# Clearing the slot rows only behind each expert's last token, and sending the last pairs' rows in one go

## What is computed

```
x = x + tanh(g0) * layernorm(attention(layernorm(x), ctx, mask))
y = layernorm(x)
logits = y @ w_router                    # 1792 tokens x 8 experts
top_vals, top_idx = top_k(logits, 2)
probs = softmax(top_vals)
h = square(relu(y @ w_fc[e]));  out_e = h @ w_proj[e]
x = x + tanh(g1) * sum over the two experts of probs * out_e
```

## Time and profile before

| | us |
|---|---|
| median of 3 runs | 1195.04 (1194.09 to 1195.85) |
| the profiled execution | 1202.38 |
| its span, first to last instruction | 1200.3 |
| PE busy | 1130.6 (94%) |
| DVE busy | 862.1 (72%) |
| ACT busy | 664.2 (55%) |
| POOL busy | 156.8 (13%) |
| mean DMA rate | 82 GB/s |

### The profile page before, as it was taken

How to read it: one execution, slowest core, us unless ns; L and a number is a source line. 1 busy time by engine, 2 the same in 40 slices (tenths; PEclk the granted TensorE clock), 3 DMA queues, 4 the chain that set the end, 5 groups by cost and what they waited for, 6 DMA issues and landing times.

```text
span 1200.3 us, 56000 instructions
## 1 busy us (share of the span) xinstructions
PE 1130.6 (94%) x24824; PEld 1082.1 (90%) x24824; DVE 862.1 (72%) x2003; ACT 664.2 (55%) x846; POOL 156.8 (13%) x186
## 2 busy tenths in 40 slices
PE   4799999999999999999999999999999999969884
PEld 4799999999999999999999999999999999968874
DVE  4467776777777776777777777777777777757677
ACT  1466565655556565656565556656565656534432
POOL 0000100010010101010111101010101101023431
PEclk9799999999999999999999999999999999989998
DMA  4223132222323233323222232323321222124306
GB/s 153 74 74 91 57 93 79 85 76 77 91 88 91 67 87 93 80 63 94 83 86 68 89 91 88 87 71 87 93 78 50 79 61 71 30 54 120 90 25 169
DMA packets 59487, 98.57 MB, mean 82 GB/s; under 512 B 14514, under 2 KB 42034, under 8 KB 59250
## 3 DMA queue, kind: packets, MB, share of 16 engines
q1 hardware_dynamic: 49538, 79.55, 23.9%
q10 hardware_dynamic: 6832, 8.92, 2.1%
q0 software_dynamic: 2880, 6.53, 1.5%
HBM read 70.32 MB, written 24.71 MB: 79 GB/s over the span
## 4 chain that ended last, share of the span: by engine, by line
PE 86%; issue 5%; DVE 5%; DMA 2%; POOL 1%; ACT 1%; SPq 0%; DVEq 0%; POOLq 0%; ACTq 0%
PE v_ps L601 22%; PE k_ps L604 21%; PE sc_ps L627 20%; PE o_ps L642 13%; PE k_ps L659 1%; PE sc_ps L544 1%; PE sc_ps L545 1%; PE k_ps L666 1%; PE sc_ps L546 1%; PE v_ps L692 1%; DVE acc L1509 1%; DVE h_sq L1438 1%; DVE acc L1452 1%; POOL rstd L460 0%; PE k_ps L805 0%
## 5 line engine op out<-in xcount | busy, mean ns | idle before, releaser
L897 ACT ACTIVATE prob<-sc_ps,m_bias 125x896 f32<-125x896 f32 x384 | 377.9, 1009 | 329.7 <-PE sc_ps L627 329.3
L601 PE MATMUL v_ps<-wv_hi,c_hi 64*125 64x256 f32 x1520 | 312.0, 285 | 2.7 <-DVE c_lo L1066 2.6
L604 PE MATMUL k_ps<-c_hi,wk_hi 64*128 64x500 f32 x760 | 306.8, 404 | 0.0
L601 PE MATMUL v_ps<-wv_lo,c_hi 64*125 64x256 f32 x1520 | 302.1, 279 | 0.0
L601 PE MATMUL v_ps<-wv_hi,c_lo 64*125 64x256 f32 x1520 | 301.9, 278 | 0.0
L604 PE MATMUL k_ps<-c_lo,wk_hi 64*128 64x500 f32 x760 | 294.0, 387 | 0.0
L604 PE MATMUL k_ps<-c_hi,wk_lo 64*128 64x500 f32 x760 | 293.2, 386 | 0.0
L1075 DVE TENSOR_TENSOR vst<-v_ps,rowv 125x512 f32<-125x512 f32 x191 | 131.3, 687 | 184.9 <-PE v_ps L601 184.9
L1277 DVE TENSOR_SCALAR prob<-prob 125x896 f32<-125x896 f32 x384 | 235.5, 626 | 21.3 <-ACT prob L897 21.1
L601 PEld LDWEIGHTS v_ps<-wv_hi,c_hi 64*125 64x125 f32 x1520 | 227.0, 185 | 16.6 <-issue 5.7
L627 PE MATMUL sc_ps<-q_hi,kh 64*125 64x224 f32 x1536 | 231.1, 268 | 7.1 <-ACT prob L897 7.1
(11 more groups left out here) (193 smaller groups left out, 1664.3 us busy)
## 6 DMA issues: line engine op xcount, KB each, us to landing
raw<-in_ctxT SPq DMA_DIRECT2D x96, 500.0 KB, 3.8
slot_rows<-zero_row SPq DMA_DIRECT2D x112, 132.0 KB, 3.7
rows<-slot_rows SPq DMA_DIRECT2D x32, 132.0 KB, 2.1
w_raw<-in_we ACTq DMA_DIRECT2D x16, 256.0 KB, 5.1
rec<-inv_scratch SPq DMA_DIRECT2D x64, 56.0 KB
expert_out<-expert_rows SPq DMA_DIRECT2D x6, 448.0 KB, 7.3
xq<-in_x ACTq DMA_DIRECT2D x16, 112.0 KB, 4.0
xr<-in_x ACTq DMA_DIRECT2D x16, 112.0 KB, 3.7
```

The lines of the kernel that those rows point to most:

```text
L601: v_last = pe.matmul(v_ps[0:TC, j * D:(j + 1) * D], c_s[v_rows, cs], w_m[v_rows, k, :], start=begin and j == 0, stop=end, skip_group_check ...
L604: k_last = pe.matmul(k_ps[:, half, 0:TG], w[k_rows, k, ws], c_m[k_rows, :], start=begin, stop=end)
L897: act.activation(prob[0:TC, c % PB, :].rearrange("p (c n) -> p c n", c=2), sc_ps[0:TC, 2 * (c % 2):2 * (c % 2) + 2, 0:NH * S // 2], ACT.Ex ...
```

## The change

- SP no longer clears the segments pair by pair. `clear_last` clears the last 128 rows of the whole tensor (what the table points at past its last tile) in pair 0 behind the load of q = 5. `clear_behind`, behind all of SP's attention work, waits for `behind_done`, reads for each expert the row behind its last token from `behind`, and clears 128 rows from there.
- DVE computes `behind` in `slots` of the last pair, on one partition, from the counts and the segments' starts.
- `send` waits no longer for `zeroed`. There are two `y_copy` buffers and a semaphore for each kind of scatter and each parity of the pair.
- In the last pair POOL does all four sends ahead of the second and third rstd; in the other pairs the order is as it was.
- `tile_table` moves from step u = 9 to u = 8, ahead of `x_after`.

```diff
+        behind = sb("behind", [P, NE], i32)
-        y_copy = sb("y_copy", [P, WR])
+        y_copy = sb("y_copy", [P, 2, WR])
-        sent = [sem(f"sent{i}") for i in range(2)]
+        sent = [[sem(f"sent{i}_{t}") for t in range(2)] for i in range(2)]
+        behind_done = sem("behind_done")
...
-            def clear_slots(i, e):
-
-                if i == 0 and e == 0:
-                    sp.wait_ge(dest_done, 2)
-                wait(sp, zeroed, 16 * (i * NE + e))
-                sp.dma_start(slot_rows[e * CAP + i * P:e * CAP + (i + 1) * P, :], zero_row[:, :]).then_inc(zeroed, 16)
+            def clear_last():
+
+                sp.wait_ge(dest_done, 2)
+                sp.dma_start(slot_rows[NE * CAP - P:NE * CAP, :], zero_row[:, :]).then_inc(zeroed, 16)
+
+            def clear_behind():
+
+                sp.wait_ge(behind_done, 1)
+                for e in range(NE):
+                    row = sp.value_load(behind[0:1, e:e + 1], min_val=0, max_val=NE * CAP - P)
+                    sp.dma_start(slot_rows[bass.ds(row, P), :], zero_row[:, :]).then_inc(zeroed, 16)
...
                     if i > 0 or q >= 2:
                         load_group(i * PG + q, q % 2)
-                    if i < CAP // P:
-                        for e in ((0, 1), (2,), (3,), (4,), (5,), (6, 7))[q]:
-                            clear_slots(i, e)
+                    if i == 0 and q == 5:
+                        clear_last()
...
             for i in range(NP):
                 pair(i)
+            clear_behind()
...
-                    sp.wait_ge(zeroed, 16 * NE * (CAP // P))
+                    sp.wait_ge(zeroed, 16 * (NE + 1))
                     for r in range(2):
-                        sp.wait_ge(sent[r], 16 * NS)
+                        for t in range(2):
+                            sp.wait_ge(sent[r][t], 8 * NS)
...
                 if r == 0:
                     pool.wait_ge(slot_done, j + 1)
-                    pool.wait_ge(zeroed, 16 * NE * min(j + 1, CAP // P))
...
-                    wait(pool, sent[1], 16 * j)
+                    wait(pool, sent[1][j % 2], 16 * (j // 2))
...
+                if i == NP - 1:
+                    for j in ranked(i):
+                        for r in range(2):
+                            send(j, r)
+                if not first:
                     inv_std(1, i - 1)
-                for j in ranked(i):
-                    send(j, 0)
+                if i < NP - 1:
+                    for j in ranked(i):
+                        send(j, 0)
                 if not first:
                     inv_std(2, i - 1)
-                for j in ranked(i):
-                    send(j, 1)
+                if i < NP - 1:
+                    for j in ranked(i):
+                        send(j, 1)
...
                     then(dve.tensor_copy(count[0:PW, :], total_ps[0:PW, :]))
+                    dve.tensor_tensor(behind[0:1, :], count[0:1, :], seg_c[0:1, :], ALU.add).then_inc(behind_done, 1)
...
                 if u == 8 and final:
                     tile_starts()
-                if u == 9 and final:
                     tile_table()
```

More of the change, by code:

```diff
@@ L453, in _ @@
             pool.memset(y_row[:, :, :], 0.0).then_inc(ones_done, 1)
-            pool.memset(y_copy[:, :], 0.0).then_inc(ones_done, 1)
+            pool.memset(y_copy[:, :, :], 0.0).then_inc(ones_done, 1)
             pool.wait_ge(ones_done, 6)
@@ L476, in send @@
                     pool.wait_ge(slot_done, j + 1)
-                    pool.wait_ge(zeroed, 16 * NE * min(j + 1, CAP // P))
                     source = y_row[0:PW, j % 2, :]
                 else:
-                    wait(pool, sent[1], 16 * j)
-                    pool.tensor_copy(y_copy[0:PW, 0:D], y_row[0:PW, j % 2, 0:D]).then_inc(copied, 1)
-                    pool.tensor_copy(y_copy[0:PW, D:D + 1].bitcast(i32), dest_i[0:PW, j, 1:2]).then_inc(copied, 1)
+                    wait(pool, sent[1][j % 2], 16 * (j // 2))
+                    pool.tensor_copy(y_copy[0:PW, j % 2, 0:D], y_row[0:PW, j % 2, 0:D]).then_inc(copied, 1)
+                    pool.tensor_copy(y_copy[0:PW, j % 2, D:D + 1].bitcast(i32), dest_i[0:PW, j, 1:2]).then_inc(copied, 1)
                     pool.wait_ge(copied, 2 * j + 2)
-                    source = y_copy[0:PW, :]
-                wait(pool, sent[r], 16 * j)
+                    source = y_copy[0:PW, j % 2, :]
+                wait(pool, sent[r][j % 2], 16 * (j // 2))
                 pool.indirect_dma_start(slot_rows[:, :], bass.IndirectOffsetOnAxis(ap=slot_i[0:PW, j, r:r + 1], axis=0),
-                                        source, None).then_inc(sent[r], 16)
+                                        source, None).then_inc(sent[r][j % 2], 16)
             def pair(i, first=False, late=False):
@@ L1155, in y_rows @@
             def y_rows(i):
-                wait(dve, sent[0], 16 * (i - 1))
+                wait(dve, sent[0][i % 2], 16 * (i // 2))
                 wait(dve, copied, 2 * (i - 1))
```

## The result

The changed kernel takes 1174.96 us (median of 4 runs, 1174.49 to 1175.2), the kernel before, run beside it, 1194.57 (4 runs): a ratio of 0.9836, 95% interval 0.9819 to 0.9853. That is 19.6 us faster. The forecast was 1177.3, a gain of 17.7, with a range from 1172.5 to 1183. The profiled execution of after took 1174.79 us, its span is 1172.5.

A forecast was written before the change was run, and what follows sets the result against it. PE was taken to bound the kernel, with two holes left, at the start and the handover. 9.1 + 8.6 = 17.7 us off the median 1195.04 gave 1177.3 us, range 1172.5 to 1183.

The forecast's parts named there:

- its two places: PE's waits: 7.14 us at the start for the first exponential, 7.75 us at the handover from attention to experts.
- Part 1, the start: Third context group's load no longer behind three clears on SP's queue: 7.1 us wait plus 2.0 lower clock, 9.1 us saved.
- The cover I named: At the start, slack before the early load would delay PE: 1 us on ACT and 4 us on the load.
- Part 1, the middle: Clears leaving SP's queue in the middle pairs gain 0, bounds 0 and 4 us; pairs stay as long as before.
- Part 2, the scatters: Last pairs' four scatters on POOL ahead of two rstd steps, with two copy buffers: 6.7 us of POOL work, nothing waits.
- Part 3, the late clears: Eight clears on SP's queue after attention take 9.0 us, landing 2.2 us before the last K and V projection ends.
- Part 4, the table: Seven table operations on DVE ahead of `x_after`, 1.2 us before a V evacuation: taken as 0, between -0.4 and +0.6.
- Handover: From attention to experts: first expert tile's next transpose 8.6 us earlier, 7.75 from PE's wait and 0.9 from the clock.
- Middle gains too: Rival, chance 0.10: removing the middle's clears gains 4 us on top, time 1173.3.
- POOL is held up by DVE: Rival, chance 0.11: scatter work on POOL stretches 2.5 times to 16.8 us, PE stalls 4.3; gain 13.4, time 1181.6.
- The early load slows its neighbours: Rival, chance 0.09: at the start the early load delays group 1's load up to 3.8 us; time 1181.1.
- The eight clears land one after another: Rival, chance 0.08: late clears on SP's queue serialise at 4.5 to 6.1 us each; time 1196.4 to 1209.

The follow-up runs named there:

- the better version: After with POOL's second-pair rstd ahead of the first expert matrix's low half: 1167.79 against 1174.64 us; also DVE's second-context-group low half ahead of K/V evacuations: 1174.02 against 1183.09.

## Why the prediction was right, point by point

**What bounds the kernel.** Right in its two places. Each was done alone, and they give 9.45 and 8.0 us of 19.6; both together, with the middle's clears left in, 18.0 and 17.8 us on two chips, against the 17.7 predicted for them.

**Part 1, the start: 9.1 predicted.** 9.45 by the times. By the traces the second `kh` comes 38.34 - 29.57 = 8.77 earlier, though PE began 19.80 - 19.36 = 0.44 later: 9.2 us between these two points, the 7.14 and a rest of 2.07, which is what was reckoned for the clock. The cover I named held: ACT's conversion was ready at 17.15 + 1.04 = 18.19, some 5 us ahead of the first scores. The load had landed by 17.15, sooner than the 18.0 that I allowed.

**Part 1, the middle: 0 predicted, about 2 found.** This is the term that was mis-sized, and the forecast of 1177.3 is 2.3 us above the result. The sign I had named, pairs as long as before, did not hold either. I had compared PE's busy share with clears (98.9%) and with almost none left (98.6%). The second stretch holds parts of two pairs and other work, so its share said nothing on the clears. The spacing of the pairs, read from one row on POOL to the next, does: 65.27 with clears and 64.77 without in the first trace. That overstates them (0.5 for 13 pairs is 6.5 us), and after has 65.04 and 64.82 at these two places on chip C with no clears at all, so 0.2 of the 0.5 belong to other work. The rest would still have shown that zero was the wrong end of my bounds 0 and 4.

**Part 2, the scatters: 6.7 us on POOL predicted, 6.3 found**, 1024.33 to 1030.66. They stand ten us earlier than the 1034 to 1042 I had named, mostly because the trace of before came from a slower kind of chip; counted from the last low half they start at 25.2 us, and the slots were known at 25.0 to 25.6 before. The sum took the mean of the scatters from `y_copy`, 1.08, for all four; the others had 1.33 in the same view. Both kinds came shorter here, 0.95 to 0.98. The first rstd wasn't made late. But of the two edits here one did all: in the new order the second copy buffer, to which the prediction gave a share, measured nothing.

**Part 3, the late clears: 9.0 us predicted, 8.93 found**, and the last had landed by 1035.0 + 3.9 = 1038.9, ahead of 1042.6. The cover held.

**Part 4, the table: 0 predicted.** PE stalls 0.46 us for the V evacuation, and its wait for the `y` row falls from 0.90 to 0.32. Counted from the last low half, the row load is issued at 1043.52 - 999.11 = 44.41 us, where I had 62.5 - 18.14 = 44.36 with the stall; but it takes 3.31 us to land where 2.07 stood in the earlier trace rows. So the 0.6 to 1.2 us that I thought to spare weren't there: PE waits 0.34 for the rows. The granted clock stayed at 1.00 behind it, and it costs nothing more, since ACT sets the pace right after.

**Handover: 8.6 predicted.** The third expert tile's transpose stands 1051.93 - 999.11 = 52.82 us behind the last low half, 1079.38 - 1018.14 = 61.24 before: 8.4 by the traces, 8.0 by the times.

**Sum.** 9.45 + 8.0 + 2.0 to 2.3 = 19.5 to 19.8, against 19.6 measured. Each of the first two has an interval of 2 us, so an agreement this close is partly luck. I had carried the gain from the profiled execution to the median unchanged, with a trace that came, by its pair lengths, from a chip on which before takes 8 us longer. The reason given was that both holes are made of waits in the program's order; that the gain hardly differs from chip to chip agrees with it: 19.9 us on chip B, 19.1 on chip C.

**The rivals.** *Middle gains too* was half right, about 2 of its 4 us.

*POOL is held up by DVE* fell: 6.3 us for what it had at 16.8. The rstd that spoke for it takes 2.00 us again at the same place, so the one row was no general price. The rule on the shared ports that I quoted for it (the Trainium skill, SBUF — State Buffer, section SBUF: two separate sides) isn't borne out for these scatters: each took 0.95 to 0.98 us while DVE was busy for 5.8 of the 7 us from 1024 to 1031. That page of the Trainium skill limits the rule to certain VectorE operations (a two-port mode, or two inputs in SBUF against a GpSimd operation that reads SBUF), a condition that the prediction left out; which of DVE's operations ran in such a mode no run shows. The copies between the scatters did stretch, to 0.63 and 0.67 us where 0.39 stood in the earlier trace rows; by what isn't shown.

*The early load slows its neighbours* fell too: ACT converts group 1 at 12.6 to 13.1 in three traces with the late load (mean 12.8) and at 12.4 to 13.6 in eleven with the early one (mean 12.8), where the rival wanted up to 3.8 later.

*The eight clears land one after another* didn't happen, and it wasn't a way to end slower: made true, it left 12.1 of the gain. Its step that failed is the price of a clear, 3.5 us and not 4.5 or more. The 4.6 from which it would be slower was a slip: by its own sum, (1069.55 + 9.1 - 1044.1) / 8, it is 4.3, and 4.6 only with the 2.4 us of the 0.2% added. And with 3.5 that sum gives a gain of 6.6, not 12.1; about 2 of the difference are the middle's, the rest stays open.

## What to carry to other kernels

Before you time an edit, ask which queue the late transfer stood in and behind what: both holes were work in program order whose inputs had long been there, and so were the two that the better version closes. Price a repeated cost by the spacing of the repeats, not by the busy share of stretches that hold different work, and compare the same repeat with and without it. And compare a trace only with times taken beside it on the same chip: 8 us lay between two kinds of chip here, about as much as each of the two holes was worth.

## What the runs showed of the hardware

The same program took 0.7% longer on some chips (or in some sessions; see above): 1183.09 us for after on chip C, 1174.64 on chip B. A pair takes 65.00 - 64.26 = 0.74 us longer there, and from 300 to 900 PE is busy for 593.4 us in the one trace and 598.4 in the other. What stands in the gaps are short stops ahead of the pv matmuls (40 stops, 12.7 us in all in that stretch, the longest 0.6, against 17 and 2.6), for which the profile names no releaser. pv is where PE issues many small instructions in a short time (64 matmuls in 1.03 us), and the page lists a DMA queue for instructions, 199 packets with 3.26 MB, 16 kB each. The Trainium skill (Runtime: NRT & Kernel Launch, section Instruction fetch mechanics) says that an engine's instructions are fetched in blocks of 16 KiB over a DMA queue of its own while it executes, and that this is mostly hidden. The size agrees. That the stops are such fetches coming late, and that the clears add to them, would fit, but no run here shows it, and it stays open.

A stop of 2.55 us that ends near 19 was followed by the lower clock in some executions and not in others of the same program. The table by stages of after on chip B, then on chip C:

```profile
20.00:25.00 5.00, 5.00 (x79) 5.00 (x77) 4.27 (x15) 3.42 (x4) 0.00 (x0) 1.00 0.26 98
...
20.00:25.00 5.00, 5.00 (x49) 5.00 (x51) 2.92 (x16) 1.01 (x1) 0.00 (x0) 0.66 0.37 106
```

It isn't the chip: on chip C the kernel with the middle's clears, whose start is the same, had 1.00 there, and on chip B the one with the late clears in a row had 0.66. The start is 1.6 us longer with the lower clock: 13.84 us from PE's 18.86 to the next resumption at 32.70 in the one, 15.41 from 19.87 to 35.28 in the other.
